# A four-layer graph network on one core: the work between its loops is arranged anew

## What is computed

```
# 0: attention without softmax, messages summed by dst
w = mlp2(edge_attr_8) + mlp2(edge_attr_16)
alpha = (q[dst] * w * k[src]).reshape(-1, 8, 8).sum(-1) * edge_weight
out = segment_sum(alpha * v[src], dst)
# 1: three steps of smoothing, norm = dinv[src] * w * dinv[dst], loops included
x = hh + proximal(spmm(x) - hh)
# 2: polynomial of degree 5 in the normalised adjacency, coefficients from a small MLP
tx = segment_sum(norm * tx[col], row); result += coeffs[k] * tx
# 3: two graph convolutions, relu between them
h = x @ W; out = segment_sum(h[src] * norm, dst) + h / deg + b
```

## Time and profile before

| | |
|---|---|
| median of three executions | 7933.46 us (7933.38 to 7944.13) |
| profiled execution, its own time | 7934.18 us |
| its span | 7932.5 us |
| mean granted TensorE clock | 0.964 |
| TensorE busy | 6931.4 us (87%) |
| VectorE busy | 5980.0 us (75%) |
| ScalarE busy | 4364.6 us (55%) |
| POOL busy | 2865.0 us (36%) |

### The profile page before, as it was taken

The page is one execution under the profiler, slowest core; times in us unless marked ns, Lnnn a source line. Parts: engine busy times, 40 slices in busy tenths (PEclk is TensorE's granted clock), DMA queues, the critical chain, the costliest instruction groups (busy, mean ns, idle before and its releaser), DMA issues. The chain is left out here.

```text
span 7932.5 us, 279512 instructions
## 1 busy us (share of the span) xinstructions
PE 6931.4 (87%) x98699; PEld 5909.3 (74%) x98724; DVE 5980.0 (75%) x17395; ACT 4364.6 (55%) x13164; POOL 2865.0 (36%) x2957
## 2 busy tenths in 40 slices
PE   2799999999999799999994888888895999998888
PEld 1455555555555599999994787788895998997878
DVE  4567776777767599898996799799898667776556
ACT  0122222222222299999994787787795666665555
POOL 0588888888878655454552000000000000000000
PEclk9999999999999999999997999999998999998889
DMA  9522222222222277676674887887895777764645
GB/s 391 164 59 60 59 61 60 59 59 60 59 60 59 64 230 232 227 230 230 229 231 156 284 298 278 284 298 280 297 334 191 200 201 201 201 195 133 175 136 162
DMA packets 656939, 1425.59 MB, mean 180 GB/s; under 512 B 284864, under 2 KB 352190, under 8 KB 653265
## 3 DMA queue, kind: packets, MB, share of 16 engines
q1 hardware_dynamic: 540674, 1232.57, 48.4%
q0 software_dynamic: 101792, 92.82, 5.6%
q10 hardware_dynamic: 13924, 93.06, 3.1%
...
## 5 line engine op out<-in xcount | busy, mean ns | idle before, releaser
L340 POOL DMA_INDIRECT sorted_rows<-sort_rows,sort_row_at x1600 | 1979.4, 1237 | 579.2 <-issue 565.2
L1603 ACT ACTIVATE smooth_msg<-smooth_ps_a,smooth_w_rows 128x64 f32<-128x64 f32 x6000 | 1311.9, 334 | 315.7 <-PE smooth_ps_a L1689 299.2
...
L1384 ACT ACTIVATE poly_cast<-poly_mat 128x1536 bf16<-128x1536 uint8 x500 | 714.8, 1475 | 445.0 <-PE poly_ps L1405 370.2
L399 PEld LDWEIGHTS sort_ps_r<-sort_count,sort_hot_dt 50*125 50x125 bf16 x1600 | 282.7, 177 | 837.1 <-issue 582.4
L413 PE MATMUL sort_ps_m<-sort_w,sort_hidden 128*125 128x64 f32 x3200 | 879.3, 430 | 0.0
L1711 PE MATMUL smooth_ps_s<-smooth_msg,smooth_hot 128*128 128x64 bf16 x7500 | 773.9, 195 | 76.2 <-DVE smooth_last_part L1842 65.4
L392 PE MATMUL sort_ps_h<-sort_attrs,sort_w 24*128 24x500 f32 x800 | 811.6, 1115 | 18.1 <-DMA sort_attrs<-in_attr_t 18.1
L1711 PE MATMUL smooth_ps_s<-smooth_rest,smooth_hot 128*128 128x64 bf16 x7500 | 769.8, 194 | 16.0 <-issue 15.9
L1711 PE MATMUL smooth_ps_s<-smooth_last_part,smooth_hot 128*128 128x64 bf16 x7500 | 768.9, 194 | 16.1 <-issue 16.1
L413 PEld LDWEIGHTS sort_ps_m<-sort_w,sort_hidden 128*125 128x125 f32 x3200 | 732.1, 320 | 41.1
L1711 PEld LDWEIGHTS smooth_ps_s<-smooth_msg,smooth_hot 128*128 128x128 bf16 x7500 | 689.0, 99 | 98.7 <-DVE smooth_last_part L1842 67.5
...
## 6 DMA issues: line engine op xcount, KB each, us to landing
poly_mat<-counts_t SPq DMA_DIRECT2D x500, 400.0 KB, 3.7
smooth_src<-src_rows SPq DMA_DIRECT2D x150, 960.0 KB, 5.0
smooth_hot<-hot_rows SPq DMA_DIRECT2D x150, 960.0 KB, 7.0
smooth_src<-src_rows SPq DMA_DIRECT2D x150, 640.0 KB, 5.7
smooth_hot<-hot_rows SPq DMA_DIRECT2D x150, 640.0 KB, 6.9
graph_edges<-sorted_rows SPq DMA_DIRECT2D x125, 700.0 KB
hot_rows<-graph_hot SPq DMA_DIRECT2D x125, 640.0 KB, 3.6
src_rows<-graph_hot_t SPq DMA_DIRECT2D x125, 640.0 KB, 3.4
```

The costliest lines, as they stand in the source:

```text
L340: pool.indirect_dma_start(out=sorted_rows, out_offset=bass.IndirectOffsetOnAxis(row_at[u][:, j:j + 1], 0), in_=rows[u][:, j, :], in_offset ...
L1384: act.activation(cast[u][h][:, DVE_S:HR, :], mat[u][h][:, DVE_S:HR, :], ACT.Copy)\
L1603: last = act.activation(at[:, i, :], ps_a[g % 2][:, i * D:(i + 1) * D], ACT.Copy, scale=w_rows[u][:, c * CHUNK + i:c * CHUNK + i + 1])
```

## The change

- `sort_edges`: SP writes the zeros of `y0_rows` at its end, out of the tile `zeros` that is there already, and waits for them. `n_spilled` is gone.
- `spill_messages`: two tiles an iteration, counted by `n_pairs`. SP loads both at once; the cast of the ids moves from VectorE to POOL; POOL issues four gathers and two scatters, and waits for each scatter. No zeros are made or written here. VectorE's and TensorE's work is the same at twice the width.
- `scale_of_degree` three times becomes `scales_of_degrees`, one block.
- `first_parts` replaces the scaling and splitting in `smooth` and the polynomial: ten blocks (640 columns) at a time, each posted by itself. In the polynomial the four first casts stand between the pieces, and the products with the coefficients come last.
- `project` becomes `conv_rows`: transposes four blocks at a time straight from `x`, products into banks of eight blocks, and the scaling and the three parts of each bank beside them, the two bfloat16 copies on ScalarE. `convolve` then posts all pairs at once.

```
@@ sort_edges, at the end of SP's program @@
+                half = YB * (D + 2) // 2
+                for h in two:
+                    by_rows(sp, y0_rows.rearrange("(p b) c -> p (b c)", b=YB)[:, h * half:(h + 1) * half],
+                            zeros[0:NL, 0:half], y0_cleared)
+                sp.wait_ge(y0_cleared, 64)
...
@@ spill_messages @@
-                sp.wait_ge(cleared, 1)
-                by_rows(sp, y_rows.rearrange("(p b) c -> p (b c)", b=YB), zeros, const)
                 with sp.Fori(0, n) as t:
-                    sp.wait_ge(added, 16 * t)
+                    sp.wait_ge(added, 32 * t)
                     sp.sem_inc(taken, 1)
-                    sp.dma_start(edges[:], sorted_rows[bass.ds(N_SLOTS + t * TE, TE), :]).then_inc(loaded, 16)
-                sp.wait_ge(added, 16 * n)
+                    load(t)
+                sp.wait_ge(added, 32 * n)
                 sp.sem_inc(taken, 1)
                 by_rows(sp, y_sb, y_rows[0:N_NODES, :].rearrange("(p b) c -> p (b c)", b=NB), y_in)
...
-                pool.memset(zeros[:], 0.0).then_inc(cleared, 1)
-                pool.wait_ge(const, 64)
+                n = count(pool)
                 with pool.Fori(0, n) as t:
+                    pool.wait_ge(got, 16 * t + 16)
+                    pool.sem_inc(taken, 1)
+                    pool.tensor_copy(from_at[:], edges[:, :, DST:SRC + 1]).then_inc(ids, 1)
                     pool.wait_ge(ids, t + 1)
                     pool.sem_inc(taken, 1)
-                    pool.indirect_dma_start(out=of_dst[:], out_offset=None, in_=qkv_rows,
-                                            in_offset=bass.IndirectOffsetOnAxis(dst_at[:, 0:1], 0)).then_inc(rows, 16)
-                    pool.indirect_dma_start(out=of_src[:], out_offset=None, in_=qkv_rows,
-                                            in_offset=bass.IndirectOffsetOnAxis(src_at[:, 0:1], 0)).then_inc(rows, 16)
+                    for i in two:
+                        for e, of in ((0, of_dst), (1, of_src)):
+                            pool.indirect_dma_start(out=of[:, i, :], out_offset=None, in_=qkv_rows,
+                                                    in_offset=bass.IndirectOffsetOnAxis(from_at[:, i, e:e + 1], 0))\
+                                .then_inc(fetched, 16)
                     pool.wait_ge(ready, t + 1)
                     pool.sem_inc(taken, 1)
...
-                    pool.wait_ge(added, 16 * t + 16)
+                    for i in two:
+                        pool.indirect_dma_start(out=y_rows, out_offset=bass.IndirectOffsetOnAxis(to[:, i:i + 1], 0),
+                                                in_=total[:, i, :], in_offset=None, compute_op=ALU.add).then_inc(added, 16)
+                        pool.wait_ge(added, 32 * t + (16 * i + 16))
+                        pool.sem_inc(taken, 1)
...
-def scale_of_degree(nc, tag, degree, extra, dinv):
+def scales_of_degrees(nc, degrees):
 
     with ExitStack() as ctx:
-        step = ctx.enter_context(Semaphores(nc))("step")
+        sem = ctx.enter_context(Semaphores(nc))
+        ready, rooted = sem("degree_ready"), sem("degree_rooted")
         with nc.Block() as blk:
             @blk.vector
             def _(dve):
-                dve.tensor_scalar(dinv[:], degree, extra, 1e-12, ALU.add, ALU.max).then_inc(step, 1)
-                dve.wait_ge(step, 2)
-                dve.reciprocal(dinv[:], dinv[:])
+                for degree, extra, inv in degrees:
+                    dve.tensor_scalar(inv[:], degree, extra, 1e-12, ALU.add, ALU.max).then_inc(ready, 1)
+                for i, (degree, extra, inv) in enumerate(degrees):
+                    dve.wait_ge(rooted, i + 1)
+                    dve.reciprocal(inv[:], inv[:])
 
             @blk.scalar
             def _(act):
-                act.wait_ge(step, 1)
-                act.activation(dinv[:], dinv[:], ACT.Sqrt).then_inc(step, 1)
+                for i, (degree, extra, inv) in enumerate(degrees):
+                    act.wait_ge(ready, i + 1)
+                    act.activation(inv[:], inv[:], ACT.Sqrt).then_inc(rooted, 1)
...
+FIRST = 10
+def first_parts(link, dve, posted, parts, xs, x, scale, rest):
+    for b in range(0, NB, FIRST):
+        at = slice(b, b + FIRST)
+        link(dve.tensor_tensor(xs[:, at], x[:, at], scale[:, at].unsqueeze(2).to_broadcast([NL, FIRST, D]), ALU.mult))
+        link(dve.tensor_copy(parts[:, at, 0, :], xs[:, at]))
+        link(dve.tensor_tensor(rest[:, at], xs[:, at], parts[:, at, 0, :], ALU.subtract))
+        link(dve.tensor_copy(parts[:, at, 1, :], rest[:, at]))
+        dve.tensor_tensor(parts[:, at, 2, :], rest[:, at], parts[:, at, 1, :], ALU.subtract).then_inc(posted, FIRST // 2)
+        yield
...
@@ spread, VectorE's program @@
-                before_vector(dve, Chain(dve, first, 0, 0))
-                dve.sem_inc(posted, PAIRS)
...
+                before = Beside(before_vector(dve, Chain(dve, first, 0, 0), posted))
                 for u in two:
                     for h in two:
+                        before.go(1)
                         cast_half(0, 0, u, h)
+                before.end()
...
@@ smooth, VectorE's program @@
-                link(dve.tensor_tensor(xs[:], x[:], wide(dinv), ALU.mult))
...
-                dve.sem_inc(posted, PAIRS)
+                for _ in first_parts(link, dve, posted, parts[0], xs, x, dinv, out):
+                    pass
...
+def conv_rows(nc, tag, x, w, dinv, xs, parts, left, ident):
+    QUAD, OCT = 4, 8
...
+        xt = [sb(f"xt{u}", [D, QUAD * NL], F32) for u in two]
+        ps_t = [pb(f"ps_t{u}", [128, 512]) for u in two]
+        ps_o = [pb(f"ps_o{u}", [128, 512]) for u in two]
...
+        quads = [slice(b, min(b + QUAD, NB)) for b in range(0, NB, QUAD)]
+        octs = [slice(b, min(b + OCT, NB)) for b in range(0, NB, OCT)]
...
+        with nc.Block() as blk:
+            @blk.tensor
+            def _(pe):
+                def products(i):
+                    pe.wait_ge(turned_sb, i + 1)
+                    o = quads[i].start // OCT
+                    if o >= 2 and quads[i].start == octs[o].start:
+                        pe.wait_ge(scaled, o - 1)
+                    for b in range(quads[i].start, quads[i].stop):
+                        at = b - octs[o].start
+                        last = nc.tensor.matmul(ps_o[o % 2][0:NL, at * D:(at + 1) * D],
+                                                xt[i % 2][:, (b - quads[i].start) * NL:(b - quads[i].start + 1) * NL], w,
+                                                start=True, stop=True, skip_group_check=True)
+                    if quads[i].stop == octs[o].stop:
+                        last.then_inc(product, 1)
+                for i, q in enumerate(quads):
+                    if i >= 2:
+                        pe.wait_ge(turned_sb, i - 1)
+                    for b in range(q.start, q.stop):
+                        last = nc.tensor.transpose(ps_t[i % 2][0:D, (b - q.start) * NL:(b - q.start + 1) * NL], x[:, b, :],
+                                                   ident[0:NL, 0:NL])
+                    last.then_inc(turned, 1)
+                    if i >= 1:
+                        products(i - 1)
+                products(len(quads) - 1)
+            @blk.scalar
+            def _(act):
+                def turn(i):
+                    act.wait_ge(turned, i + 1)
+                    act.activation(xt[i % 2][:, 0:size(quads[i]) * NL], ps_t[i % 2][0:D, 0:size(quads[i]) * NL], ACT.Copy)\
+                       .then_inc(turned_sb, 1)
+                def first(o):
+                    act.wait_ge(scaled, o + 1)
+                    act.activation(parts[:, octs[o], 0, :], xs[:, octs[o], :], ACT.Copy).then_inc(firsts, 1)
+                def second(o):
+                    act.wait_ge(rests, o + 1)
+                    act.activation(parts[:, octs[o], 1, :], left[:, octs[o], :], ACT.Copy).then_inc(seconds, 1)
+                n = len(octs)
+                for i in range(n + 3):
+                    for j in (2 * i, 2 * i + 1):
+                        if j < len(quads):
+                            turn(j)
+                    if 0 <= i - 2 < n:
+                        first(i - 2)
+                    if 0 <= i - 3 < n:
+                        second(i - 3)
+            @blk.vector
+            def _(dve):
+                def scale(o):
+                    dve.wait_ge(product, o + 1)
+                    s = octs[o]
+                    dve.tensor_tensor(xs[:, s, :], ps_o[o % 2][0:NL, 0:size(s) * D].rearrange("p (b d) -> p b d", d=D),
+                                      dinv[:, s].unsqueeze(2).to_broadcast([NL, size(s), D]), ALU.mult).then_inc(scaled, 1)
+                def rest(o):
+                    dve.wait_ge(firsts, o + 1)
+                    dve.tensor_tensor(left[:, octs[o], :], xs[:, octs[o], :], parts[:, octs[o], 0, :], ALU.subtract)\
+                       .then_inc(rests, 1)
+                def last_part(o):
```

(22 more changed lines are left out.)

191 lines of the change are left out of this document (71 added, 120 removed).

## The result

The changed kernel takes 7890.32 us (median of five executions, 7879.35 to 7895.18), the kernel before beside it 7933.46 (7922.65 to 7944.34). The ratio is 0.9941, with a 95% interval of 0.9926 to 0.9956. The profiled execution took 7890.32 us around a span of 7888.5, against 7934.18 around 7932.5: 44.0 us less of span. The forecast was 51.0 us less and 7882.5 us, with a range of 7869 to 7900. The number lies inside, but its parts don't add up as they were forecast, and the stage table shows it. A stage runs from SP's first issue in a block, or from an instruction named there, to the next such mark, in both traces.

A forecast was written before the change was run, and what follows sets the result against it. Between the long loops TensorE stands nearly still and each block starts where the one before stops, so savings there count: 14.6 + 2.1 - 1.0 + 0.5 + 10.2 + 24.6 = 51.0 us off 7933.46 gives 7882.5 us, range 7869 to 7900.

The forecast's parts named there:

- Spilled edges: Graph's spill block: earlier load, two tiles per iteration and zeros written in the sort fetch the sums 14.6 us earlier.
- Degrees: Degree scaling before smoothing: one block takes 2.1 us instead of 4.2 for three, 2.1 us less.
- Smoothing's first parts: Entry of smoothing: five instructions become 25 smaller ones, taking 18.0 us; together 1.0 us slower, bounds 0 and +3.
- Polynomial: Entry of the polynomial: first parts in pieces before the coefficient products, 0.5 us less, bounds -2.5 and +2.
- Rows of the convolutions: `conv_rows` replacing `project`: quads of 2.9 us end each block 5.1 us earlier, 10.2 us for two.
- Start of the convolutions: First parts lie under the products; the first matrix's cast sets TensorE's start, 12.5 and 12.1 us earlier, 24.6 together.
- So nothing is lost by these rows: Convolution start: 6.4 MB pass in 19 us at 334 GB/s, before TensorE asks for the last matrices at about 23.
- signs of being wrong: TensorE idle ahead of `conv_cast` for `conv_mat` in pairs two and three, a quad over 3.6 us, low clock beyond first pair.
- second rival: Convolution start: zeros, table and matrices move at 200 GB/s, not 334, 9 us more than covered, twice; 7900 us, chance 0.12.
- main case: Whole kernel: the sum of terms comes as forecast, 7875 to 7891 us, chance 0.58.
- slower rival (the clock stays low): Loop entries: TensorE stays at 1.2 GHz for whole rows, 4.2 us more each; 7937 us and more, chance 0.04.

## Why the prediction was right, step by step

- **Spilled edges: right** (14.1 for 14.6). Its load was priced by the row of one without a write beside it (1.9 us); for two tiles at once it took 2.9. That beside a write the same load takes 6.6, so that 4.7 us of the term hung on this, I had not seen.
- **Degrees: right** in mechanism. The block is shorter by 2.6 us, not 2.1, since the reciprocals follow at 0.35 us instead of 0.5.
- **Smoothing's first parts: right** (-0.6 for -1.0): 25 instructions took the 18.0 us forecast. With one piece it is 17.75 us, so pieces are a small loss.
- **Polynomial: near in its number, wrong in its cause.** 1.1 us for 0.5. I had drawn up a balance in which pieces about pay for themselves; in fact they cost 3.6, and the coefficients' place gains 3.3 to 4.7 (31.0 or 32.5 to 27.8). Between the single traces of before and after the two nearly cancel.
- **Rows of the convolutions: the mechanism right, the term too small**, 15.5 for 10.2. In the first block TensorE's part took 35.3 us (36.4 forecast), the start came 0.5 sooner than forecast, the tail took 3.5 (4.4 between the two times forecast), and the way into the next block was 0.4 shorter: 2.9 us together, and the second block is alike.
- **Start of the convolutions: right** (23.8 for 24.6): the first matrix's cast sets it.
- **"So nothing is lost by these rows": wrong, by 19.3 us.** This is the step that failed. It took 334 GB/s, the rate of 8 us in which the table and matrices moved, over the whole stretch, and asked for one deadline only. That rate didn't fit the zeros at all: in the kernel that writes them in `conv_rows`, the write alone, with nothing moved beside it, takes 15.7 us at 104 GB/s:

```profile
7299.40:7315.10 15.70, 15.70 (x68) 12.59 (x67) 2.07 (x3) 4.33 (x8) 1.28 (x1) 0.50 0.29 104
```

  Windows of after, from SP's first issue to the zeros' landing, and the stretch of before that answers to it, up to the table's landing:

```profile
7331.00:7366.00 35.00, 23.96 (x255) 22.42 (x255) 12.59 (x16) 16.07 (x12) 2.43 (x3) 0.85 0.79 254
```
```profile
7362.70:7390.60 27.90, 9.29 (x95) 9.08 (x96) 17.96 (x9) 5.71 (x4) 2.32 (x2) 0.61 0.67 231
```

At 254 GB/s the 6.4 MB take 25 us, and the fourth matrix of pair two was indeed there for its cast at 7357.08, 25 us behind SP's first load; the zeros were not, but landed at 7364.91. But TensorE asks for each half row by itself: it ran out at 7353.7, while the cast of the third matrix, which had to land first, starts on ScalarE only at 7354.69 and ends when TensorE goes on, at 7356.2. And the spill chain, which waits for the zeros themselves, stood in no line of the sum. Two of the signs of being wrong that the prediction lists came with it: TensorE idle ahead of `conv_cast` for want of a matrix in pair two, and a low clock beyond the first pair. The **second rival** had this mechanism and its size (9 us each); the runs show 8.3 as a mean, of which 1.8 are the clock. The main case held the number only since this loss was covered by a term for the rows that was 5.3 too small, and by 6.6 us of unchanged stages: luck, as far as the number goes.
- **The unchanged stages** were no term at all. Over thirteen traces the sort ended at 2739.2 to 2753.9 us, smoothing's loop took 1715.9 to 1729.1 and the polynomial's 1125.5 to 1134.2. That is the scatter of a run, and one trace against another can carry 6 us of it and more.
- **The slower rival (the clock stays low)** did not come as it was put: the clock is back at 2.4 GHz inside the first pair of each convolution, and no row of 50 products is low from end to end. But it falls again behind waits. In the first convolution it holds through the 2.50 us wait and is low behind the 7.34 at the spill product; in the second it is low behind the waits of 2.75, 6.99 and 3.56 us, and 4.2 us of that loop's 12.6 are this. The prediction's reasoning on the clock stopped at the entry of a loop.

The Trainium skill (DMA: Bandwidth & Descriptors, section Issuing engines are not separate DMA queues) says that transfers of all issuing engines interleave on the same 16 DMA engines. The trace agrees: zeros issued by POOL slowed matrices issued by SP, and were themselves 32 us on the way instead of 19.3 (four matrices beside them) and 15.7 (nothing beside them).
